# Attention scores from two float32r parts in four row groups, with two banks for the maxima and three for the exponentials

## The reference

```python
q = jnp.einsum('bsd,hde->bhse', x, wq) + bq
k = jnp.einsum('bsd,hde->bhse', x, wk) + bk
v = jnp.einsum('bsd,hde->bhse', x, wv) + bv
scale = 1.0 / jnp.sqrt(jnp.asarray(q.shape[-1], q.dtype))
scores = jax.nn.softmax(jnp.einsum('bhse,bhte->bhst', q, k) * scale, axis=-1)
att = jnp.einsum('bhst,bhte->bhse', scores, v)
```

## Time and profile before

| | before |
|---|---|
| median of 3 runs | 1170.81 us (1170.74 to 1175.88) |
| the profiled execution's own time | 1174.08 us |
| its span, first to last instruction | 1172.4 us |
| mean granted TensorE clock | 0.901 |
| PE busy | 981.7 us, 84% of the span |
| DVE busy | 766.4 us, 65% |
| ACT busy | 579.6 us, 49% |
| POOL busy | 444.3 us, 38% |

### The profile page before, as it was taken

One profiled execution on the slowest core, in us unless ns is written; L12 is line 12 of the kernel. 1 busy time (PEld: TensorE's weight loads), 2 busy tenths in 40 slices (PEclk: granted clock), 3 DMA queues, 4 the chain that ended last, 5 costly groups with the idle time before them and its releaser, 6 DMA issues.

```text
span 1172.4 us, 21238 instructions
## 1 busy us (share of the span) xinstructions
PE 981.7 (84%) x6249; PEld 616.0 (53%) x6249; DVE 766.4 (65%) x1912; ACT 579.6 (49%) x1225; POOL 444.3 (38%) x625
## 2 busy tenths in 40 slices
PE   4699999999899999994198999999996539999764
PEld 3133333333233333332197888889885439999621
DVE  3668787878687878896188756665665336656333
ACT  1057676767576767771023533552453116666421
POOL 4030414131222222121324565665534336666532
PEclk9569999999899999996599999999998559999876
DMA  4432323232232324510600010100101012222232
GB/s 141 140 120 75 132 72 131 74 128 76 100 105 97 106 96 108 186 49 10 277 19 19 20 31 27 31 26 22 33 8 48 18 33 68 65 68 68 82 92 75
DMA packets 55645, 90.11 MB, mean 77 GB/s; under 512 B 9393, under 2 KB 40539, under 8 KB 54902
## 3 DMA queue, kind: packets, MB, share of 16 engines
q1 hardware_dynamic: 45942, 58.68, 17.5%
q0 software_dynamic: 9600, 30.24, 7.2%
HBM read 49.62 MB, written 39.30 MB: 76 GB/s over the span
## 4 chain that ended last, share of the span: by engine, by line
PE 34%; DVE 6%; DMA 3%; issue 3%; POOL 3%; ACT 3%; SPq 0%; DVEq 0%; ACTq 0%; POOLq 0%
PE a L2030 6%; PE tb L1860 5%; PE a L1852 4%; PE a L1870 4%; PE b_ L2039 3%; PE c L1826 2%; PE a L2039 2%; PE b_ L1826 2%; DMA weights<-back_dram 1%; DMA xg<-tokens_dram,row_of 1%; PE b_ L1922 1%; PE b_ L1821 1%; ACT L1418 1%; PE b_ L1914 1%; POOL rows_dram L1303 1%
## 5 line engine op out<-in xcount | busy, mean ns | idle before, releaser
L630 DVE TENSOR_REDUCE nmax<-ps_s 128x1 f32<-128x512 f32 x512 | 324.8, 683 | 87.7 <-PE ps_s L795 86.5
L524 ACT ACTIVATE p_ring<-ps_t 128x512 f32<-128x512 f32 x512 | 287.2, 597 | 141.6 <-PE ps_t L806 138.1
L817 PE MATMUL ps_av<-p_ring,v_ext 128*32 128x512 f32 x1024 | 138.8, 615 | 0.0
L795 PE MATMUL ps_s<-weights 72*128 72x512 bf16 x256 | 108.3, 427 | 19.5 <-DMA weights<-q_parts_dram 15.6
L1466 ACT ACTIVATE weights<-a,wtile 128x128 f32<-128x128 f32 x288 | 82.3, 368 | 49.5 <-PE a L2030 49.5
L1330 POOL DMA_INDIRECT back_dram<-weights,target x72 | 84.0, 1167 | 57.8 <-DVE weights L1783 51.9
L806 PE MATMUL ps_t<-weights 75*128 75x512 bf16 x256 | 102.0, 398 | 2.6 <-ACT p_ring L524 1.5
L806 PE MATMUL ps_t<-q_stack,k_stack 75*128 75x512 bf16 x256 | 96.7, 382 | 3.9 <-ACT p_ring L524 2.0
L795 PE MATMUL ps_s<-k_stack,q_stack 72*128 72x512 bf16 x256 | 98.1, 383 | 1.3 <-DVE nmax L630 1.3
L1374 ACT ACTIVATE hid<-a 128x512 f32<-128x512 f32 x64 | 38.2, 597 | 112.5 <-PE a L1852 112.3
L1303 POOL DMA_INDIRECT rows_dram<-hrow,slot x64 | 63.2, 988 | 64.5 <-DVE slot L1690 46.1
(11 more groups left out here) (286 smaller groups left out, 1681.2 us busy)
## 6 DMA issues: line engine op xcount, KB each, us to landing
rows_dram<-wmod POOLq DMA_DIRECT2D x8, 2145.0 KB
q_parts_dram<-q_parts SPq DMA_DIRECT2D x40, 128.0 KB, 2.4
xt<-rows_dram SPq DMA_DIRECT2D x72, 65.0 KB, 1.8
weights<-k_parts_dram SPq DMA_DIRECT2D x16, 288.0 KB
weights<-q_parts_dram SPq DMA_DIRECT2D x16, 288.0 KB
k_stack<-k_parts_dram SPq DMA_DIRECT2D x16, 288.0 KB
q_stack<-q_parts_dram SPq DMA_DIRECT2D x16, 288.0 KB
wall<-in_wall SPq DMA_DIRECT2D x1, 4112.0 KB, 20.7
```

The costliest lines, as they stand in the source:

```text
L524: nc.scalar.activation(probs[:, u % RING, :], ps_t[u % TBANKS][:], ACT.Exp, scale=HD ** -0.5).then_inc(exp_done, 1)
L630: nc.vector.tensor_reduce(nmax[:, js, n:n + 1], ps_s[u % SBANKS][:], AX.X, ALU.max, negate=True).then_inc(max_done, 1)
L795: nc.tensor.matmul(ps_s[u % SBANKS][:], q_stack[par][0:STACK, h, quarter(t)], k_stack[par][0:STACK, h, :], start=True, stop=True).then_inc ...
L817: last = nc.tensor.matmul(ps_av[32 * g:32 * (g + 1), :], v_ext[par][:, t, HG * j + g, :], probs[:, (HG * k + g) % RING, :], start=(t == 0) ...
```

## The change

1. **Parts.** Q and K are split into two float32r parts (float32 with a short mantissa): part 0 is ACT's rounded value, part 1 the remainder, which the DVE writes itself. POOL's `split` is gone. Three products stay (K parts 0, 0, 1 with Q parts 0, 1, 0), so a head's stack has 24 rows.
2. **Row groups.** Head g of a group of four lies in partitions 32g to 32g + 23, with the maxima's two rows behind them. score(u) uses the head (u + 2) mod 4 and score_t(u) the head u mod 4, so neighbouring matmuls are in different row groups.
3. **Banks.** Two `ps_s` and three `ps_t`.
4. **Maxima.** Two parts: POOL has two instructions instead of four, the transpose is of float32 instead of bf16, and SP has two DMAs instead of one.
5. **DMAs.** 3 + 3 saves of 256 KB, 8 loads of 24 partitions x 8 KB. All K loads wait for the K saves alone, and the first score of a batch waits for all eight loads (one semaphore `stack_in`).
6. **Memory.** The stacks have memory of their own, POOL fills both K stacks with ones at the start, and the load of the expert weights doesn't wait for the last stack's use any more.

```diff
-PARTS = 3
-TERMS = PARTS * PARTS
-STACK = TERMS * HD
+PARTS = 2
+K_SLOTS = (0, 0, 1)
+Q_SLOTS = (0, 1, 0)
+SLOTS = len(K_SLOTS)
+STACK = SLOTS * HD
 MROW = STACK
+GROUP = P // HG
-SBANKS, TBANKS = 3, 2
-QSLOTS = 5
+SBANKS, TBANKS = 2, 3
+def head_of_score(v):
+    return (v + 2) % HG
...
             def move_maxima(bb, j, par):
                 sp.wait_ge(m_rows_ready[j], bb + 1)
-                sp.dma_start(q_stack[par][MROW:MROW + PARTS, HG * j:HG * (j + 1), :],
-                             m_rows[:, j, :]).then_inc(m_in[j], 16)
+                for c in range(PARTS):
+                    sp.dma_start(q_stack[par][MROW + c:P:GROUP, j, :],
+                                 m_rows[HG * NT * c:HG * NT * (c + 1), j, :]).then_inc(m_in[j], 16)
...
+            def load_stacks(stack, dram, par):
+                for g in range(HG):
+                    sp.dma_start(stack[par][GROUP * g:GROUP * g + STACK, :, :],
+                                 window(dram, T * g, [[H * T, STACK], [HG * T, NG], [1, T]])).then_inc(stack_in, 16)
...
-                nc.gpsimd.tensor_copy(parts[:, 1, :], rest[:]).then_inc(second, 1)
-                pool.wait_ge(second, bb + 1)
-                nc.gpsimd.tensor_tensor(parts[:, 2, :], rest[:], parts[:, 1, :], ALU.subtract).then_inc(third, 1)
...
                     dve.wait_ge(first, nxt + 1)
-                    dve.wait_ge(third, nxt)
-                    nc.vector.scalar_tensor_tensor(rst[:], bank[:], bias[:], parts[:, 0, :], ALU.add, ALU.subtract
-                                                   ).then_inc(ready, 1)
+                    nc.vector.scalar_tensor_tensor(parts[:, 1, :], bank[:], bias[:], parts[:, 0, :].bitcast(F32),
+                                                   ALU.add, ALU.subtract).then_inc(second, 1)
...
             def score(bs, js, v, u, par):
-                if v == 0:
-                    pe.wait_ge(stack_in[js], 32 * (bs + 1))
+                if js == 0 and v == 0:
+                    pe.wait_ge(stack_in, 16 * 2 * HG * (bs + 1))
...
-                h, t = HG * js + v % HG, v // HG
-                nc.tensor.matmul(ps_s[u % SBANKS][:], q_stack[par][0:STACK, h, quarter(t)], k_stack[par][0:STACK, h, :],
-                                 start=True, stop=True).then_inc(s_filled, 1)
+                first, t = GROUP * head_of_score(v), v // HG
+                rows_ = slice(first, first + STACK)
+                nc.tensor.matmul(ps_s[u % SBANKS][:], q_stack[par][rows_, js, quarter(t)].bitcast(F32R),
+                                 k_stack[par][rows_, js, :].bitcast(F32R), start=True, stop=True).then_inc(s_filled, 1)
...
-                nc.tensor.matmul(ps_t[u % TBANKS][:], k_stack[par][0:STACK + PARTS, h, quarter(t)],
-                                 q_stack[par][0:STACK + PARTS, h, :], start=True, stop=True).then_inc(t_filled, 1)
+                rows_ = slice(GROUP * g, GROUP * g + STACK + PARTS)
+                nc.tensor.matmul(ps_t[u % TBANKS][:], k_stack[par][rows_, j, quarter(t)].bitcast(F32R),
+                                 q_stack[par][rows_, j, :].bitcast(F32R), start=True, stop=True).then_inc(t_filled, 1)
```

More of the change, by code:

```diff
@@ L260, in program_attention @@
         k_saved = sem("k_saved")
-        stack_in = [sem(f"stack_in{j}") for j in range(NG)]
+        stack_in = sem("stack_in")
         s_filled = sem("s_filled")
@@ L407, in iteration @@
                     move_maxima(b, 2, par)
-                if it.after:
-                    load_stacks(2, 1 - par)
-                    load_stacks(3, 1 - par)
                 if it.here:
@@ L431, in _ @@
         def _(pool):
[L432 removed]
             nc.gpsimd.memset(half[:], -0.5).then_inc(consts, 1)
             for i in range(2):
+                nc.gpsimd.memset(k_stack[i][:], 1.0).then_inc(consts, 1)
+            for i in range(2):
                 nc.gpsimd.memset(v_ext[i][:], 0.0).then_inc(consts, 1)
[L436 removed]
+                pool.wait_ge(consts, 4 + 2 * i)
                 nc.gpsimd.memset(v_ext[i][:, :, :, HD:HD + 1], 1.0).then_inc(consts, 1)
[L439 to L446 removed]
             def maxima(bb, j):
[L450 removed]
                 pool.wait_ge(max_done, UNITS * bb + HG * NT * (j + 1))
@@ L552, in first_part @@
                 def first_part(which):
-                    filled, saved, slots, parts, bank, bias, ready = {
-                        "q": (q_filled, q_saved, QSLOTS, q_parts, bank_a, bq, q1_ready),
-                        "k": (k_filled, k_saved, PARTS, k_parts, bank_b, bk, k1_ready)}[which]
+                    filled, saved, parts, bank, bias, ready = {
+                        "q": (q_filled, q_saved, q_parts, bank_a, bq, q1_ready),
+                        "k": (k_filled, k_saved, k_parts, bank_b, bk, k1_ready)}[which]
                     act.wait_ge(filled, nxt + 1)
-                    act.wait_ge(saved, 16 * slots * nxt)
+                    act.wait_ge(saved, 16 * SLOTS * nxt)
                     act.wait_ge(wqkv_in, 96)
@@ L673, in rest @@
                 def rest(which):
-                    bank, bias, parts, rst, first, ready, third = {
-                        "q": (bank_a, bq, q_parts, q_rest, q1_ready, q_rest_ready, q3_ready),
-                        "k": (bank_b, bk, k_parts, k_rest, k1_ready, k_rest_ready, k3_ready)}[which]
+                    bank, bias, parts, first, second = {
+                        "q": (bank_a, bq, q_parts, q1_ready, q2_ready),
+                        "k": (bank_b, bk, k_parts, k1_ready, k2_ready)}[which]
                     dve.wait_ge(first, nxt + 1)
-                    dve.wait_ge(third, nxt)
-                    nc.vector.scalar_tensor_tensor(rst[:], bank[:], bias[:], parts[:, 0, :], ALU.add, ALU.subtract
-                                                   ).then_inc(ready, 1)
+                    nc.vector.scalar_tensor_tensor(parts[:, 1, :], bank[:], bias[:], parts[:, 0, :].bitcast(F32),
+                                                   ALU.add, ALU.subtract).then_inc(second, 1)
                 def values():
```

116 lines of the change are left out of this document (37 added, 79 removed).

## The result

| | before | after |
|---|---|---|
| median of runs | 1173.35 us (1170.74 to 1176.06, 4 runs) | 1365.10 us (1353.50 to 1381.44, 4 runs) |
| ratio | | 1.1601, 95% interval 1.1515 to 1.1687 |
| span of the profiled execution | 1172.4 us | 1351.8 us |
| granted TensorE clock, mean | 0.901 | 0.730 |

The account below looks back on a forecast made before the run. Neither PE nor DVE alone was the bound; they hold each other up around the weigh. 1174.1 - 6.6 at full clock + 29 for clock falls gave 1196.5 profiled, so 1193 as median; 8-in-10 range 1150 to 1262 us.

Parts of the forecast that it names:

- the clock term: Attention: a fifth of the 446 us from 76 to 522 at half clock, 90 us x 0.32 = +29 us.
- The analogy with the expert part: Attention: full-array jobs and weighs bring the clock back, as they do behind the falls in the expert part.
- the prediction's own 32%: Attention: a stretch at half clock loses 32% of its length, a batch taking 87.5 us in place of 59.3.
- +3 and -4: Full-clock attention: +3 us over 7 batches (59.3 against 58.9 each), -4 us in the last half batch.
- Steady group at full clock: Attention's plain group of four units: 3.21 us against 3.18, the missing third bank taking what faster products give.
- Jobs on the full array: Batch's 13 jobs between row groups: 0.1 us per change on both sides as a bound, about +18 us with paired overlap.
- Distance of two starts: Score products on row groups: starts 0.14 us apart, the weight load's pace, bounded by almost nothing and 0.43.
- Prologue: Before attention: last Q part at 19.23, first score at 30.5 in place of 39.00, then 32 scores at 0.69 each.
- the -8.5 and +2.9: Prologue: first score 8.5 us earlier, then 32 scores without exponentials slower by 0.09 each, +2.9 us.
- Last half batch: End of attention, no maxima: three banks let score_t start earlier, 8 x 0.5 = -4 us, groups of 2.6.
- half clock throughout: Rival: attention at half clock all the time, 1164 + 210 = 1374 us, chance 0.04.
- The five falls behind 33-row products: Expert part: clock falls behind matmuls on 33 rows, the sign held against the rival that the clock stays.

Follow-up runs that it names:

- the run with few rows: Kernel before with only the first of three K parts in the stack (24 rows, 27 with the maxima), bf16, same banks: 1477.69 us.
- one full-array product at each place: Changed kernel with three and two banks, one added 128-row product ahead of the third and fourth unit's score of each four: 1324.95 us.

## Why the prediction was wrong

The step that failed is the size of the clock term: "I take a fifth of the 446 us". It was four fifths. The reason given for a fifth, that "the jobs on 128 rows and the weighs stay and bring it back", is refuted: they are there in every batch, and the run with few rows stayed at the lower clock for 156 us with all of them in it. In the attention of the changed kernel, too, the stays at the lower clock last 24 to 82 us but for one of 14, and those at the upper one 3 to 20 us. The analogy with the expert part, where a fall was over within some 3 us, misled: behind the two thin products of that stretch the next work is on the full array. PE also waited there (0.70 us ahead of the second), so those falls did not show rows and idle time apart.

The mechanism and, nearly, its price held. By the prediction's own 32% the 526 us at half clock (80% of 657.2) cost 168 us, and attention would be 657 - 168 = 489 us at full clock, against 471 by the prediction's sum (471.6 before, +3 and -4). An estimate for the 18 us left is the group: 4.76 us in place of the 4.58 reckoned, 0.18 us in each of some 100 groups at half clock (there are 120, and jobs take a part of the 526 us), 18 us. Of this, 0.19 are the distance from a score to its maximum, taken from bf16 rows (0.64) and in truth 0.83 at half clock, and 0.15 that from a score_t to the weigh (0.57, in truth 0.72); 0.14 go the other way, since the products start together.

The rest, point by point:

- *Steady group at full clock*: 3.31 with a transpose job, measured 3.38. The sum of 3.21 puts score_t(3) 0.10 us behind score(3) where the text's own pace is 0.14; with that it is 3.25, some 4 us more over 7 batches. That the bank split gives back what the row groups win is shown from both sides: alone it costs about 2.7 us a batch (61.6 against 58.9), and with the old split the groups take 3.13.
- *Jobs on the full array*: the upper bound had 0.1 us on both sides of a job. Between bf16 products on 24 or 48 rows a transpose pays 0.09 us ahead and 0.15 behind; in the changed kernel it was not taken apart.
- *Distance of two starts*: 0.14 us taken, the load's pace; measured 0.00 to 0.01 across row groups behind a weigh. It decides little, as foreseen, since the banks decide.
- *Prologue*: the last Q part was ready at 18.85 (predicted 19.23), but the first score started at 34.52, not 30.5. I had added 1 us for more bytes of the stacks. But the tail took 15.7 us where it took 10.0, and the DMA engines moved 192 GB/s in it, some 3.0 MB, where they had moved 160 GB/s, 1.6 MB (estimates from the two stretches below, first before, then after). The old tail stood in a quiet stretch, and the new one begins 10 us earlier, while more is moved. The prediction's sum took the same tail for granted. The loads of the Q stacks are issued behind those of the K stacks, the last at some 27.8; which of the two made the delay was not tested. Then 0.79 us a score (1.57 for two) in place of 0.69. The first score_t came at 59.77 against 59.39: the -8.5 and +2.9 came to +0.4 instead of -5.6.

```profile
29.01:39.00 9.99, 0.00 (x0) 0.00 (x1) 0.00 (x0) 0.00 (x0) 0.00 (x0) 0.50 0.56 160
18.85:34.52 15.67, 2.73 (x20) 1.89 (x21) 5.42 (x15) 0.00 (x0) 1.71 (x2) 0.65 0.74 192
```

- *Last half batch*: 703.82 - 701.22 = 2.60 us at full clock, as written (2.6); but it is one of few: others ran at half clock, and that gain went too (from 706.61 to the next weigh at 710.97 is one of 4.36 us).
- *Rivals*: "half clock throughout", 1374 us with a chance of 0.04, is nearest to what came. It deserved far more. The five falls behind 33-row products were what the trace had on few rows and the clock, and I gave half of the chance to a number in between that no row supported.
- *What I passed over*: the fall in the attention of the kernel before. It was named as a dip and not looked into; PE had waited for ACT and the DVE right ahead of it.

What stays open: how much PE's idle time does beside the rows (the new bank split alone brought more falls on 72 rows; the changed kernel with the old split has a higher clock and is busier), how the 90 us of the bank split divide, and why one full-array product at each place did so badly with the old split.

## What to carry to other kernels

Before products are cut to few rows of the array, or spread over row groups, look for falls of the granted clock behind thin products and behind waits anywhere in the trace, look at the clock first when such a kernel has run, and weigh the saving against the whole stretch at the lower level. Give a bank away only where the trace shows that nobody waits for it: here a third score bank was worth more than the row groups. And where a state of the chip is not understood, give its far end a real chance instead of a middle value that no row supports.

## What the runs showed that I had not expected

- Products on 24 to 27 rows lower the granted clock although PE shows as busy for 433 of 435 us: 0.57 over 65 to 500 us against 0.98 with 72 and 75 rows, and 0.87 with 48 and 51.
- Four more products on 128 rows for every four units made the changed kernel 110 us faster; the same four on 24 rows made it 14 us faster, less than its runs differ among themselves.
- A transpose job on the full array between bf16 products on 24 to 51 rows costs 0.24 us more than between products on 72 and 75 (at full clock 0.31 + 0.59 us against 0.22 + 0.44).
- Row groups: four float32r products of 512 columns start within 0.01 us behind a weigh and last 0.49 us each at full clock and 0.79 at half, where bf16 takes 0.38 and 0.61 to 0.63. The Trainium skill, TensorE: Matmul & The Clock Gate, section Why this matters for your kernels, has row groups start together within 4 ns; the trace, which shows hundredths, agrees.
- The runs of the changed kernel spread over 28 us, those of the kernel before over 5 (four runs each).
